# Two FFNs and linear attention on one core: expert coefficients moved by a unit, three chunks' queries taken from split z, state mask moved

## The chip, the cores and the metric

The kernel runs on one core of a Trainium2 chip. Its time is the device time of one execution in microseconds (us). Five engines work side by side and meet at semaphores: TensorE (PE, matmuls and, as PEld, weight loads), VectorE (DVE), ScalarE (ACT), GpSimd (POOL) and SyncE (SP), which issues DMAs.

## The reference, cut to what matters

Four blocks follow each other, each on a layer norm of the running sum `x` (4 x 1024 tokens of 256 numbers): a state space block, an FFN with product keys, a linear attention, and the same FFN again.

```
x = x + mamba(layernorm(x))
x = x + ffn(layernorm(x))
x = x + attn(layernorm(x))
x = x + ffn(layernorm(x))

ffn: queries = (z @ W_q).reshape(2, n, 64)           # n = 4096 tokens
     routing = einsum('tnd,tdk->tnk', queries, keys)   # top 8 of 64 keys, twice
     scores, indices = top 8 of the 64 sums
     ew  = silu(z . down_embed[indices]) * softmax(scores)
     out = (silu(z @ gate_w) * (z @ up_w)) @ down_w + ew @ up_embed[indices]

attn: q, k = relu(z @ Wq) / 4, relu(z @ Wk) / 4;  v = z @ Wv;  u = silu(z @ Wu)
      kv  = k^T v per head (16 heads of 16)
      out = (srms_norm(q kv) * u) @ Wo
```

The reshape to (2, n, 64) is what couples the chunks: the first half of all tokens gives the first key half's queries, the second half the others.

## The kernel before, in words

`res` holds `x` in SBUF throughout. An FFN works on eight chunks (`c`) of 512 tokens. `z` is the normalised and transposed chunk in two parts, a rounded high part and the rest, so that a product takes three fast matmuls (`split_mm`, format fp32r) for each block of 128 rows.

A chunk has twelve units (`i`, KM = 12). Units 0 to 7 (KH = 8) are hidden columns: PE makes the gate (psG) and the up projection (psU), ACT the silu, DVE the product (`product`, L1412), ACT rounds it (`high`, L1276), DVE makes the rest (`low`, L1417). Units 8 to 11 are the 512 experts: gate is the product with down_embed, and into psU PE transposes the expert coefficients C (L1197). The two buffers of psG, psU, sil and prod alternate. Then the down projection (L1234) runs in two halves, and DVE adds each to `res` (L1459). Behind the first half PE turns the next chunk's z (`turn`).

The coefficients come about beside units 0 to 7. Route scores are made from `qs` behind unit 0, DVE finds the highest (`highest`), ACT makes the exponentials at unit 3, DVE normalises them (`normalise_softmax`), POOL spreads them over 8 x 64 (W, L1108), and DVE masks W and corrects one entry (`coefficients`: four L1397, L1404, L1405), which raises C_ready. On DVE this stood behind `product(6)` and `low(5)`:

```
for i in range(KM):
    product(c, i)
    if i > 0: low(c, i - 1)
    ...
    if i == KH - 2: coefficients(c)
```

The queries of chunk pair s and s + 4 serve the routes of chunks 2s and 2s + 1. Chunks 0, 1, 4 and 5 of the first FFN and 0 and 4 of the second have theirs made by the block before. The others are asked inside earlier chunks (table ASKED): DVE normalises the chunk once more (`question`), PE turns it at unit 1 (L1167, eight transposes), ACT copies it (L1291), PE multiplies with W_q at unit 3 in full precision (`asked`, L1172, two matmuls of 512 columns), and ACT keeps the result in QT. The buffers lie in W's space, so that POOL's W waits for the question.

The chunks with a question were loops on PE, ACT and partly POOL, those without another loop, the last ones straight code.

In attention a looped sequence on DVE (`sequence`) gates and squares two halves, scales the first (`scale(b, 0)`, L1872), scales the second, which waits for POOL's inverse norms (L1601), and masks the next sequence's state to its heads (`keep_kv`, L1851). PE waits for that state ahead of output 0 (L1706), since output and state share the accumulator `acc`.

Of the kernel before, what the change touches and what calls it, by code (L numbers as in the profile page):

```python
# [14 lines left out]
P = 128  # L15
# [955 lines left out]
class Between:  # L971


    def __init__(self, nc, sb):
        at = nc.sbuf_base
        self.SW = sb("SW", [P, 2, TILES * TOP * KEYS])
        self.z = nc.alloc_sbuf_tensor_at("z_att", [P, 2, KD, SEQ], FP32R, offset=at)
        self.zn = sb("zns", [P, 2, TILES, D])


# [24 lines left out]
def ffn(nc, res, dram, name, shared, between, norms, first, out=None):  # L1005

    ASKED = {1: 2, 2: 6, 3: 3, 4: 7} if first else {0: 1, 1: 5, 2: 2, 3: 6, 4: 3, 5: 7}
    ctx = ExitStack()  # L1010
    with ctx:
# [18 lines left out]
        top1 = sb("top1", [P, TILES, 2, TOP])  # L1030
        sums = sb("sums", [P, TILES, TOP, TOP])
        top2 = sb("top2", [P, TILES, TOP])
# [57 lines left out]
        def _(pool):  # L1090
# [6 lines left out]

            def chunk(c, n=None):
# [6 lines left out]
                if n is not None:  # L1105
                    pool.wait_ge(q_full, n + 1)
# [14 lines left out]
            if first:  # L1121
                low(2)
                chunk(0)
                pool.wait_ge(C_ready, 1)
                low(3)
                inverse(2, 1)
                inverse(3, 2)
                chunk(1, 0)
                inverse(6, 3)
                chunk(2, 1)  # L1130
                inverse(7, 4)
                with pool.Fori(3, 5) as c:
                    chunk(c, c - 1)
                with pool.Fori(5, CHUNKS) as c:
                    chunk(c)
                pool.wait_ge(next_var, 1)
                at = slice(0, SEQ_TILES)
                pool.tensor_tensor(norms.inv[:, at, 0], norms.var[:, at], mhalf[:, 0:SEQ_TILES],
                                   ALU.pow).then_inc(next_inv, 1)
            else:  # L1140
                chunk(0, 0)
# [3 lines left out]
                with pool.Fori(1, 6) as c:  # L1145
                    chunk(c, c)
                with pool.Fori(6, CHUNKS) as c:
                    chunk(c)

        @block.tensor  # L1150
        def _(pe):
# [22 lines left out]

            def turn(c, n):

                pe.wait_ge(zn_ready, c)
                if n is not None:
                    pe.wait_ge(QT_ready, n + 1)
                turned(psX, zn).then_inc(turn_full, 1)  # L1180
# [19 lines left out]

            def chunk(c, more, n=None):
                pe.wait_ge(z_ready, c + 1)
                start = first and isinstance(c, int) and c == 0
                for i in range(KM):
# [3 lines left out]
                    if i == 0:  # L1208
# [7 lines left out]
                        last.then_inc(route_full, 1)  # L1216
                    if i == 1 and n is not None:
                        pe.wait_ge(zq_ready, n + 1)
                        pe.wait_ge(Rt_ready, c + 1)
                        turned(psX, zq).then_inc(turnq_full, 1)  # L1220
                    if i == 3 and n is not None:
                        pe.wait_ge(zT_ready, n + 1)
                        asked(psX[:, 0, :], zT).then_inc(q_full, 1)
                if start:
                    pe.wait_ge(w_low, 2)
                for i in range(2):
# [13 lines left out]
                    if i == 0 and more:  # L1240
                        turn(c + 1, n)

            if first:
                chunk(0, True)
                with pe.Fori(1, 5) as c:
                    chunk(c, True, c - 1)
                with pe.Fori(5, CHUNKS - 1) as c:
                    chunk(c, True)
            else:
                with pe.Fori(0, 6) as c:  # L1250
                    chunk(c, True, c)
                chunk(6, True)
            chunk(CHUNKS - 1, False)

        @block.scalar
        def _(act):
# [20 lines left out]

            def chunk(c, more, n=None, k=None):
                for i in range(KM):
# [9 lines left out]
                    if i == 2 and k is not None:  # L1289
                        act.wait_ge(turnq_full, n + 1)  # L1290
# [4 lines left out]
                    if i == 4 and k is not None:  # L1295
                        act.wait_ge(q_full, n + 1)
                        keep(k, psX[:, 0, :])
                    if i == 6 and first and not more:
# [9 lines left out]
                if more:  # L1308
                    prepare(c + 1, None if k is None else n + 1)
                    high_z(c + 1)  # L1310

            if first:
                prepare(0, None)
                chunk(0, True)
                with act.Fori(0, 2) as b:
                    chunk(2 * b + 1, True, 2 * b, b + 2)
                    chunk(2 * b + 2, True, 2 * b + 1, b + 6)
                with act.Fori(5, CHUNKS - 1) as c:
                    chunk(c, True)
            else:  # L1320
                prepare(0, None)
                with act.Fori(0, 3) as b:
                    chunk(2 * b, True, 2 * b, b + 1)
                    chunk(2 * b + 1, True, 2 * b + 1, b + 5)
                chunk(6, True)
            chunk(CHUNKS - 1, False)

        @block.vector
        def _(dve):
# [90 lines left out]
            def chunk(c, more, prepare=None, early=None):  # L1420
                for i in range(KM):
# [47 lines left out]
            if first:  # L1469
                def start_second():  # L1470
                    statistics(2)
                    statistics(3)
                    question(2, 0, 1)

                def start_third():
                    statistics(6)
                    question(6, 1, 3)

                def start_fourth():
                    statistics(7)  # L1480
                    question(3, 2, 2)

                chunk(0, True, start_second)
                chunk(1, True, start_third)
                chunk(2, True, start_fourth)
                chunk(3, True, lambda: question(7, 3, 4))
                chunk(4, True)
                with dve.Fori(5, CHUNKS - 1) as c:
                    own.enter(c - 5, 9)
                    chunk(c, True)  # L1490
                    own.leave(CHUNKS - 6)
            else:
                def late_statistics():
                    own.link(token_statistics(nc, own, norms, res, stats, mv4, pause, CHUNKS - 1))
                    nc.vector.tensor_scalar(norms.var[:, LATE_TILES], norms.mv[:, LATE_TILES, 1], EPS, None,
                                            ALU.add).then_inc(var_ready, 1)

                question(1, 0, None)
# [5 lines left out]
                chunk(5, True)  # L1504
                chunk(6, True)
            chunk(CHUNKS - 1, False)
# [7 lines left out]
def attention(nc, res, dram, norms, shared, between):  # L1514
# [5 lines left out]
    with ctx:  # L1520
# [303 lines left out]
        def _(dve):  # L1824
# [203 lines left out]
```

## Time and profile before

| | us |
|---|---|
| median of 3 runs | 1921.82 |
| lowest, highest | 1918.57, 1923.24 |
| the profiled execution, its own time | 1917.6 |
| its span in the profile | 1915.9 |
| mean granted clock of TensorE | 0.971 |

A timeline row gives start, duration, engine, line, operation and tiles (written <- read), how many instructions of one kind it merges, and in brackets the engine's idle time ahead of it and what ended that. Matmuls are pipelined: their durations overlap, and their pace is to be read from the starts. In a table by stretch the granted clock is a share of 2.4 GHz. The state space block ends some 912 us into the span, the first FFN at 1318, attention at 1508.

### The profile page before, as it was taken

To read this page: it belongs to the slowest core of one execution; us is meant where nothing else is said; L and a number is where in the kernel's file an instruction comes from. 1 tells how busy PE (TensorE), PEld (TensorE's weight loads), DVE (VectorE), ACT (ScalarE), POOL (GpSimd) and SP (SyncE) were. 2 spreads that over 40 slices of the span, in tenths; PEclk is the share of its full clock that TensorE was granted. 3 is DMA by queue.
4 is the path that set the end of the run, shared out by engine and by line. 5 is a ranking of instruction groups with operands and counts; after the bars stand their busy time and mean duration, and the time that the engine had idled before them with its cause. 6 is when DMAs were issued, how large, how long until landed. Compare 5 with 4: busy or idle time off the path is not lost. (4 is left out here: it accounts for less than half of the span.)

```text
span 1915.9 us, 26914 instructions
## 1 busy us (share of the span) xinstructions
PE 1756.1 (92%) x9643; PEld 1385.4 (72%) x9643; DVE 1435.7 (75%) x2217; ACT 1083.5 (57%) x1870; POOL 1061.3 (55%) x633
## 2 busy tenths in 40 slices
PE   6888989898998989767999999999999899999999
PEld 2556666665656666656788888888888688888888
DVE  4799999999999999999766656664444755555565
ACT  6777786878787876777344333342333443333433
POOL 3889999999999999999511111111445411111011
PEclk9898999999999999889999999999999999999999
DMA  6223332333333332261000000000000000000000
GB/s 195 85 80 106 100 100 94 95 105 92 105 92 102 104 101 92 79 208 50 1 1 1 0 0 1 1 22 6 1 0 1 1 11 11 11 11 11 11 12 12
DMA packets 59091, 101.11 MB, mean 53 GB/s; under 512 B 11120, under 2 KB 11248, under 8 KB 58864
## 3 DMA queue, kind: packets, MB, share of 16 engines
q1 hardware_dynamic: 58992, 99.88, 16.6%
q8 instruction: 51, 0.84, 0.2%
q14 instruction: 48, 0.39, 0.1%
HBM read 95.14 MB, written 4.72 MB: 52 GB/s over the span
## 5 line engine op out<-in xcount | busy, mean ns | idle before, releaser
L383 POOL TENSOR_TENSOR m_U<-m_U,m_C 128x1024 f32<-128x1024 f32 x255 | 600.8, 2369 | 25.7 <-DVE m_U L890 15.5
L525 PEld LDWEIGHTS m_y<-ident,m_U 128*128 128x128 f32 x2048 | 252.4, 148 | 118.1 <-issue 70.9
L890 DVE TENSOR_TENSOR_SCAN m_U<-m_dA,m_carry,m_U 128x512 f32<-128x512 f32 x256 | 311.4, 1272 | 5.2 <-ACT m_dA L758 4.8
L525 PE MATMUL m_y<-ident,m_U 128*128 128x128 f32 x2048 | 284.7, 285 | 30.4 <-POOL m_U L383 30.3
L890 DVE TENSOR_TENSOR_SCAN m_U<-m_dA,m_U 128x512 f32<-128x512 f32 x256 | 296.5, 1209 | 11.5 <-ACT m_dA L758 8.2
L758 ACT ACTIVATE m_dA<-high,m_negA 128x512 f32<-128x512 f32 x256 | 172.4, 685 | 71.5 <-DVE m_U L890 71.0
L758 ACT ACTIVATE m_dA<-even,m_negA 128x512 f32<-128x512 f32 x256 | 170.7, 684 | 54.1 <-DVE m_U L890 53.0
L1102 POOL TENSOR_TENSOR SW<-g_Rt 128x1024 f32<-128x1024 f32 x16 | 31.6, 1997 | 258.3 <-ACT g_Rt L1287 258.3
L1282 ACT ACTIVATE g_sil<-g_psG 128x512 f32<-128x512 f32 x96 | 57.6, 600 | 156.1 <-PE g_psG L1161 155.9
L1282 ACT ACTIVATE f_sil<-f_psG 128x512 f32<-128x512 f32 x96 | 57.5, 599 | 151.3 <-PE f_psG L1161 150.8
L1102 POOL TENSOR_TENSOR SW<-f_Rt 128x1024 f32<-128x1024 f32 x16 | 31.6, 1997 | 190.6 <-ACT f_Rt L1287 190.6
L506 PE MATMUL m_psB<-m_stack,m_pick 128*128 128x512 f32 x196 | 100.7, 514 | 35.0 <-DVE m_U L873 34.6
L873 DVE TENSOR_TENSOR m_U<-even,m_psB 128x1024 f32<-128x1024 f32 x100 | 120.3, 1203 | 11.2 <-PE m_psB L506 11.0
L1161 PE MATMUL f_psG<-zs,weights_hi 128*128 128x512 f32 x384 | 124.3, 405 | 2.5 <-DVE f_pause L1468 2.5
L1161 PE MATMUL g_psG<-zs,weights_hi 128*128 128x512 f32 x384 | 124.7, 406 | 1.4 <-DVE g_pause L1468 1.4
L873 DVE TENSOR_TENSOR m_U<-high,m_psB 128x1024 f32<-128x1024 f32 x96 | 115.6, 1204 | 4.2 <-PE m_psB L506 4.2
L415 PE MATMUL m_job<-turned 128*128 128x512 f32 x224 | 107.6, 603 | 3.8 <-issue 3.5
L1412 DVE TENSOR_TENSOR zns<-g_psU,g_sil 128x512 f32<-128x512 f32 x96 | 66.3, 690 | 59.6 <-PE g_psU L1161 50.8
L1234 PE MATMUL f_psO<-weights_hi,f_H_hi 128*128 128x256 f32 x384 | 109.2, 284 | 0.4 <-POOL weights_lo L1116 0.3
L1234 PE MATMUL g_psO<-weights_hi,g_H_hi 128*128 128x256 f32 x384 | 108.8, 283 | 0.0
L1234 PE MATMUL g_psO<-weights_lo,g_H_hi 128*128 128x256 f32 x384 | 107.3, 280 | 0.0
L1234 PE MATMUL f_psO<-weights_lo,f_H_hi 128*128 128x256 f32 x384 | 107.3, 280 | 0.0
(369 smaller groups left out, 4383.2 us busy)
## 6 DMA issues: line engine op xcount, KB each, us to landing
m_C<-bc_rows SPq DMA_DIRECT2D x256, 256.0 KB, 3.2
m_B<-bc_rows SPq DMA_DIRECT2D x60, 256.0 KB, 3.6
even<-in_ffn_w SPq DMA_DIRECT2D x16, 256.0 KB, 4.9
out<-res SPq DMA_DIRECT2D x8, 512.0 KB, 2.8
res<-in_x SPq DMA_DIRECT2D x1, 3072.0 KB, 13.4
res<-in_x SPq DMA_DIRECT2D x2, 512.0 KB, 4.3
turned<-in_Wkvqu SPq DMA_DIRECT2D x1, 1024.0 KB, 4.8
high<-in_in_w SPq DMA_DIRECT2D x1, 512.0 KB, 4.6
```

What stands on the lines that cost most here:

```text
L383: pool.tensor_tensor(u, u, C[:, M % C_RING, :].unsqueeze(1).to_broadcast([P, PE_E, CHUNK]), ALU.mult).then_inc(hc_ready, 1)
L415: ins = nc.tensor.matmul(out, w, x, start=first and k == 0, stop=last and k == len(pairs) - 1)
L506: nc.tensor.matmul(psB[:, :], pick[:, n:n + 1].to_broadcast([P, P]), stack[:, q, :], start=True, stop=True).then_inc(B_full, 1)
L525: last = nc.tensor.matmul(y[:, t, j * P:(j + 1) * P], U[:, M % U_RING, j, t * P:(t + 1) * P], ident[:, :], start=False, stop=n == N - 1, i ...
L758: nc.scalar.activation(dA[:, s % A_RING, :], delta[q][:, e, :], ACT.Exp, scale=negA[:, e, n:n + 1]).then_inc(dA_ready, 1)
L873: nc.vector.tensor_tensor(U[:, M % U_RING, :, :], dx[q][:, pair(p), :], psB[:, :].unsqueeze(1).to_broadcast([P, PE_E, CHUNK]), ALU.mult).t ...
L890: nc.vector.tensor_tensor_scan(u, dA[:, s % A_RING, :], u, carry[:, e, n:n + 1] if q else 0.0, ALU.mult, ALU.add).then_inc(scan_done, 1)
L1102: pool.tensor_tensor(S[:, 2 * b:2 * b + 2, :, :], Rt[:, b, 0, :, 0:TOP].unsqueeze(3).to_broadcast([P, 2, TOP, KEYS]), Rt[:, b, 1, :, :].un ...
L1161: last = nc.tensor.matmul(out, a, b, start=n == 0, stop=n == len(terms) - 1)
L1234: last = nc.tensor.matmul(psO[:, i, h * D:(h + 1) * D], H[a][:, k, j * P:(j + 1) * P], lower[b][:, k, :], start=m == 0, stop=m == len(term ...
L1282: nc.scalar.activation(sil[:, i % 2, :], psG[:, i % 2, :], ACT.Silu).then_inc(g_free, 1)
L1412: nc.vector.tensor_tensor(prod[:, i % 2, :], psU[:, i % 2, :], sil[:, i % 2, :], ALU.mult).then_inc(u_free, 1)
```

## The change

1. `coefficients(c)` on DVE stands behind `product(5)` and `low(4)`.
2. Questions: three chunks' queries in the second FFN (1, 2, 3) and two in the first (2, 3) are made while that chunk is worked on, from its own z parts: six split matmuls (`asked_own`) behind unit 5 into psX's second bank, copied by ACT at unit 6. W_q gets a high and a low part for it once (`wqs`). The others (6, 7 in the first FFN; 5, 6, 7 in the second) are still turned.
3. Chunks 0 to 4 are written out on PE, ACT and POOL; a loop runs over 5 and 6. `sums` uses the space of `qs`. Statistics and inverse roots of the first FFN's later chunks are made in another order.
4. In attention the mask of the state stands between the two scalings.

```diff
-    ASKED = {1: 2, 2: 6, 3: 3, 4: 7} if first else {0: 1, 1: 5, 2: 2, 3: 6, 4: 3, 5: 7}
+    TURNED = {1: 6, 3: 7} if first else {1: 5, 3: 6, 4: 7}
+    OWN = (2, 3) if first else (1, 2, 3)
+    BEHIND = 5
...
+            def asked_own(out):
+                terms = [(between.wqs[:, i, k, :], z[j][:, k, :]) for k in range(KD) for i, j in ((0, 0), (0, 1), (1, 0))]
+                for n, (a, b) in enumerate(terms):
+                    last = nc.tensor.matmul(out, a, b, start=n == 0, stop=n == len(terms) - 1)
+                return last
...
-                    if i == 3 and n is not None:
-                        pe.wait_ge(zT_ready, n + 1)
+                    if i == 3 and turns(c):
+                        pe.wait_ge(zT_ready, turned_in(c) + 1)
                         asked(psX[:, 0, :], zT).then_inc(q_full, 1)
+                    if i == 5 and own_asks(c):
+                        asked_own(psX[:, 1, :]).then_inc(q_full, 1)
...
+            for c in range(BEHIND):
+                chunk(c, True)
+            with pe.Fori(BEHIND, CHUNKS - 1) as c:
+                chunk(c, True)
             chunk(CHUNKS - 1, False)
...
+                    if i == 6 and own_asks(c):
+                        act.wait_ge(q_full, asked_in(c + 1))
+                        keep(c, psX[:, 1, :])
...
+                nc.scalar.activation(between.wqs[:, 0, :, :], wq, ACT.Copy)
...
-                    if i == KH - 2:
+                    if i == KH - 3:
                         coefficients(c)
...
+                def low_wq():
+                    dve.wait_ge(qs_ready, 1)
+                    nc.vector.tensor_tensor(between.wqs[:, 1, :, :], wq, between.wqs[:, 0, :, :].bitcast(FP32),
+                                            ALU.subtract)
...
+                def end_first():
+                    statistics_of(2, 6)
+                    question(6, 0, 2)
+
+                chunk(0, True, end_first, low_wq)
+                chunk(1, True, lambda: statistics_of(3, 7))
+                chunk(2, True, lambda: question(7, 1, 4), lambda: dve.wait_ge(inv_ready, 3))
...
-                question(1, 0, None)
-                chunk(0, True, lambda: question(5, 1, 1), late_statistics)
-                chunk(1, True, lambda: question(2, 2, None))
-                chunk(2, True, lambda: question(6, 3, None))
-                chunk(3, True, lambda: question(3, 4, None))
-                chunk(4, True, lambda: question(7, 5, None))
+                chunk(0, True, lambda: question(5, 0, 1), late_statistics)
+                chunk(1, True)
+                chunk(2, True, lambda: question(6, 1, None))
+                chunk(3, True, lambda: question(7, 2, None))
...
                 scale(b, 0)
+                keep_kv(b + 1)
                 scale(b, 1)
-                keep_kv(b + 1)
```

How it stands on the engines. DVE in a chunk of the second FFN, units 4 to 7, before (L1412 is `product`, L1417 `low`, L1397 to L1405 `coefficients`):

```order
L1412 TENSOR_TENSOR zns<-g_psU,g_sil 128x512
L1417 TENSOR_TENSOR g_H_lo<-zns,g_H_hi 128x512
L1412 TENSOR_TENSOR zns<-g_psU,g_sil 128x512
L1417 TENSOR_TENSOR g_H_lo<-zns,g_H_hi 128x512
L1412 TENSOR_TENSOR zns<-g_psU,g_sil 128x512
L1417 TENSOR_TENSOR g_H_lo<-zns,g_H_hi 128x512
L1397 SCALAR_TENSOR_TENSOR SW,g_csum<-SW,g_top 128x512 x4
L1404 TENSOR_TENSOR SW<-SW,g_csum 128x4
L1405 TENSOR_SCALAR SW<-SW 128x4
L1412 TENSOR_TENSOR zns<-g_psU,g_sil 128x512
```

The same stretch after (L1429 is now `product`, L1434 `low`, L1414 to L1422 `coefficients`):

```order
L1429 TENSOR_TENSOR zns<-g_psU,g_sil 128x512
L1434 TENSOR_TENSOR g_H_lo<-zns,g_H_hi 128x512
L1429 TENSOR_TENSOR zns<-g_psU,g_sil 128x512
L1434 TENSOR_TENSOR g_H_lo<-zns,g_H_hi 128x512
L1414 SCALAR_TENSOR_TENSOR SW,g_csum<-SW,g_top 128x512 x4
L1421 TENSOR_TENSOR SW<-SW,g_csum 128x4
L1422 TENSOR_SCALAR SW<-SW 128x4
L1429 TENSOR_TENSOR zns<-g_psU,g_sil 128x512
L1434 TENSOR_TENSOR g_H_lo<-zns,g_H_hi 128x512
```

One pair of product and low, that of units 6 and 5, has moved from ahead of the coefficients to behind them.

DVE in the looped attention sequence, before:

```order
L1844 TENSOR_TENSOR z_att<-a_acc,z_att 128x512
L1876 ISA
L1872 TENSOR_TENSOR a_og<-a_og,a_rinv 128x256 x4
L1876 REGISTER_ALU
L1877 REGISTER_ALU
L1872 TENSOR_TENSOR a_og<-a_og,a_rinv 128x256 x4
L1849 REGISTER_ALU
L1851 TENSOR_TENSOR a_kvh<-a_acc,a_same_head 128x128 x2
L1883 ISA
```

And after:

```order
L1891 ISA
L1887 TENSOR_TENSOR a_og<-a_og,a_rinv 128x256 x4
L1864 REGISTER_ALU
L1866 TENSOR_TENSOR a_kvh<-a_acc,a_same_head 128x128 x2
L1891 REGISTER_ALU
L1892 REGISTER_ALU
L1887 TENSOR_TENSOR a_og<-a_og,a_rinv 128x256 x4
L1898 ISA
```

The two masking instructions stand ahead of the second four scalings.

## Rows read from the trace of the kernel before

**Rows 1.** The page's first part: busy us (share), instructions; one line of it.

```profile
PE 1756.1 (92%) x9643; PEld 1385.4 (72%) x9643; DVE 1435.7 (75%) x2217; ACT 1083.5 (57%) x1870; POOL 1061.3 (55%) x633
```

**Rows 2.** Groups of instructions on PE: busy us, mean ns, idle before and releaser.

```profile
L1197 PE MATMUL g_psU<-ident,SW 128*128 128x128 f32 x128 | 19.4, 274 | 4.4 <-DVE SW L1405 4.4
```

**Rows 3.** Timeline of PE, second FFN, chunk 1: start us, duration us, instruction.

```profile
1585.13 0.62 PE L1161 MATMUL g_psG<-zs,weights_hi 128*128 128x512 f32 x2
...
1586.26 0.39 PE L1161 MATMUL g_psG<-zs,weights_lo 128*128 128x512 f32 x1
1587.20 0.63 PE L1197 MATMUL g_psU<-ident,SW 128*128 128x128 f32 x4 [0.55 <-DVE SW L1405]
...
1588.83 0.40 PE L1161 MATMUL g_psG<-zs,weights_lo 128*128 128x512 f32 x1
1589.06 0.60 PE L1197 MATMUL g_psU<-ident,SW 128*128 128x128 f32 x4
```

**Rows 4.** Timeline of DVE at the same place.

```profile
1580.91 0.68 DVE L1417 TENSOR_TENSOR g_H_lo<-zns,g_H_hi 128x512 fp32r<-128x512 f32 x1
1582.66 0.69 DVE L1412 TENSOR_TENSOR zns<-g_psU,g_sil 128x512 f32<-128x512 f32 x1 [1.07 <-PE g_psU L1161]
...
1583.87 0.74 DVE L1397 SCALAR_TENSOR_TENSOR SW<-SW,g_top 128x512 f32<-128x512 f32 x1
...
1586.88 0.17 DVE L1405 TENSOR_SCALAR SW<-SW 128x4 f32<-128x4 f32 x1
```

**Rows 5.** Timeline of POOL, then of DVE, first FFN, chunk 6.

```profile
1233.98 3.63 POOL L1108 TENSOR_TENSOR SW<-f_ex 128x2048 f32<-128x2048 f32 x1 [5.82 <-DVE f_ex L1390]
...
1235.79 2.36 DVE L1417 TENSOR_TENSOR f_H_lo<-zns,f_H_hi 128x512 fp32r<-128x512 f32 x1
...
1238.89 0.68 DVE L1417 TENSOR_TENSOR f_H_lo<-zns,f_H_hi 128x512 fp32r<-128x512 f32 x1
```

**Rows 6.** Timeline of PE: first coefficient transposes of five chunks.

```profile
1195.92 0.63 PE L1197 MATMUL f_psU<-ident,SW 128*128 128x128 f32 x4 [0.55 <-DVE SW L1405]
...
1244.45 0.63 PE L1197 MATMUL f_psU<-ident,SW 128*128 128x128 f32 x4 [0.55 <-DVE SW L1405]
...
1536.00 0.63 PE L1197 MATMUL g_psU<-ident,SW 128*128 128x128 f32 x4 [0.55 <-DVE SW L1405]
...
1840.51 0.63 PE L1197 MATMUL g_psU<-ident,SW 128*128 128x128 f32 x4 [0.55 <-DVE SW L1405]
...
1889.04 0.63 PE L1197 MATMUL g_psU<-ident,SW 128*128 128x128 f32 x4 [0.55 <-DVE SW L1405]
```

**Rows 7.** Timeline of PE, then of DVE, attention, around output 0.

```profile
1365.96 0.71 PE L1644 MATMUL a_acc<-a_kv 128*128 128x128 f32 x4
...
1370.04 6.68 PE L1706 MATMUL a_acc<-a_wo,a_ogT 128*128 128x256 f32 x16 [2.92 <-DVE a_kvh L1851]
...
1412.72 0.71 PE L1644 MATMUL a_acc<-a_kv 128*128 128x128 f32 x4
...
1417.09 5.36 PE L1706 MATMUL a_acc<-a_wo,a_ogT 128*128 128x256 f32 x16 [3.22 <-DVE a_kvh L1851]
...
1458.43 0.71 PE L1644 MATMUL a_acc<-a_kv 128*128 128x128 f32 x4
...
1462.41 3.72 PE L1706 MATMUL a_acc<-a_wo,a_ogT 128*128 128x256 f32 x16 [2.84 <-DVE a_kvh L1851]
...
1367.98 1.43 DVE L1872 TENSOR_TENSOR a_og<-a_og,a_rinv 128x256 f32<-128x256 f32 x4 [9.06 <-POOL a_rinv L1601]
1369.33 0.48 DVE L1851 TENSOR_TENSOR a_kvh<-a_acc,a_same_head 128x128 f32<-128x128 f32 x2
```

**Rows 8.** Busy time by stretch: us; PE, PEld, DVE, ACT, POOL; granted clock; DMA.

```profile
1370.00:1377.00 7.00, 6.96 (x18) 5.64 (x19) 0.81 (x2) 0.00 (x0) 0.00 (x0) 0.57 0.00 0
```

**Rows 9.** Timeline of POOL, first FFN, end of chunk 0.

```profile
956.72 1.25 POOL L1096 TENSOR_TENSOR inv<-var,f_mhalf 128x4 f32<-128x4 f32 x1 [1.09 <-DVE var L1347]
```

**Rows 10.** Who waited for whom: us in total, times, longest us.

```profile
DVE res L1459 <- PE f_psO L1234: 75.3, 14, 6.3
```

More of the change, by code:

```diff
@@ L978, in __init__ @@
         self.zn = sb("zns", [P, 2, TILES, D])
+        self.wqs = sb("wqs", [P, 2, KD, P], FP32R)
 class Norms:
@@ L1005, in ffn, with turned_in, asked_in, asks @@
 def ffn(nc, res, dram, name, shared, between, norms, first, out=None):
-    ASKED = {1: 2, 2: 6, 3: 3, 4: 7} if first else {0: 1, 1: 5, 2: 2, 3: 6, 4: 3, 5: 7}
+    TURNED = {1: 6, 3: 7} if first else {1: 5, 3: 6, 4: 7}
+    OWN = (2, 3) if first else (1, 2, 3)
+    BEHIND = 5
+    def turned_in(c):
+        return len([b for b in TURNED if b < c])
+    def asked_in(c):
+        return turned_in(c) + len([b for b in OWN if b < c])
+    def asks(c):
+        return isinstance(c, int) and (c in TURNED or c in OWN)
+    def turns(c):
+        return isinstance(c, int) and c in TURNED
+    def own_asks(c):
+        return isinstance(c, int) and c in OWN
     ctx = ExitStack()
@@ L1096, in inverse, with chunk @@
                 pool.tensor_tensor(norms.inv[:, at, 0], norms.var[:, at], mhalf[:, 0:TILES], ALU.pow).then_inc(inv_ready, 1)
-            def chunk(c, n=None):
+            def chunk(c):
                 pool.wait_ge(Rt_ready, c + 1)
@@ L1126, in _ @@
                 inverse(2, 1)
[L1127 to L1130, printed above, removed]
+                inverse(6, 2)
+                chunk(1)
+                inverse(3, 3)
                 inverse(7, 4)
-                with pool.Fori(3, 5) as c:
-                    chunk(c, c - 1)
-                with pool.Fori(5, CHUNKS) as c:
+                for c in range(2, BEHIND):
+                    chunk(c)
+                with pool.Fori(BEHIND, CHUNKS) as c:
                     chunk(c)
@@ L1140, in _ @@
             else:
-                chunk(0, 0)
+                chunk(0)
                 pool.wait_ge(var_ready, 1)
@@ L1144, in _ @@
                                    ALU.pow).then_inc(inv_ready, 1)
-                with pool.Fori(1, 6) as c:
-                    chunk(c, c)
-                with pool.Fori(6, CHUNKS) as c:
+                for c in range(1, BEHIND):
+                    chunk(c)
+                with pool.Fori(BEHIND, CHUNKS) as c:
                     chunk(c)
@@ L1173, in asked, with turn @@
                 return last
-            def turn(c, n):
+            def asked_own(out):
[3 more added lines that the diff above has]
+                return last
+            def turn(c):
                 pe.wait_ge(zn_ready, c)
-                if n is not None:
-                    pe.wait_ge(QT_ready, n + 1)
+                if isinstance(c, int) and asks(c - 1):
+                    pe.wait_ge(QT_ready, asked_in(c))
                 turned(psX, zn).then_inc(turn_full, 1)
@@ L1199, in hidden, with chunk @@
                 last.then_inc(u_full, 1)
-            def chunk(c, more, n=None):
+            def chunk(c, more):
                 pe.wait_ge(z_ready, c + 1)
@@ L1240, in chunk @@
                     if i == 0 and more:
[L1241 to L1252, printed above, removed]
+                        turn(c + 1)
+            for c in range(BEHIND):
+                chunk(c, True)
+            with pe.Fori(BEHIND, CHUNKS - 1) as c:
+                chunk(c, True)
             chunk(CHUNKS - 1, False)
@@ L1276, in high, with chunk @@
                 nc.scalar.activation(H[0][:, i, :], prod[:, i % 2, :], ACT.Copy).then_inc(hi_ready, 1)
-            def chunk(c, more, n=None, k=None):
+            def chunk(c, more):
                 for i in range(KM):
@@ L1288, in chunk @@
                                              ACT.Copy).then_inc(Rt_ready, 1)
-                    if i == 2 and k is not None:
-                        act.wait_ge(turnq_full, n + 1)
+                    if i == 2 and turns(c):
+                        act.wait_ge(turnq_full, turned_in(c) + 1)
                         nc.scalar.activation(zT, psX[:, :, :], ACT.Copy).then_inc(zT_ready, 1)
@@ L1294, in chunk @@
                         nc.scalar.activation(ex[:, :, :], ex[:, :, :], ACT.Exp).then_inc(exp_ready, 1)
-                    if i == 4 and k is not None:
-                        act.wait_ge(q_full, n + 1)
-                        keep(k, psX[:, 0, :])
+                    if i == 4 and turns(c):
+                        act.wait_ge(q_full, asked_in(c) + 1)
+                        keep(TURNED[c], psX[:, 0, :])
+                    if i == 6 and own_asks(c):
+                        act.wait_ge(q_full, asked_in(c + 1))
+                        keep(c, psX[:, 1, :])
                     if i == 6 and first and not more:
@@ L1308, in chunk @@
                 if more:
-                    prepare(c + 1, None if k is None else n + 1)
+                    prepare(c + 1, asked_in(c + 1) if asks(c) else None)
                     high_z(c + 1)
             if first:
[L1313 to L1325, printed above, removed]
+                nc.scalar.activation(between.wqs[:, 0, :, :], wq, ACT.Copy)
+            prepare(0, None)
+            for c in range(BEHIND):
+                chunk(c, True)
+            with act.Fori(BEHIND, CHUNKS - 1) as c:
+                chunk(c, True)
             chunk(CHUNKS - 1, False)
@@ L1469, in _, with statistics_of @@
             if first:
[L1470 to L1486, printed above, removed]
+                def low_wq():
+                    dve.wait_ge(qs_ready, 1)
+                    nc.vector.tensor_tensor(between.wqs[:, 1, :, :], wq, between.wqs[:, 0, :, :].bitcast(FP32),
+                                            ALU.subtract)
+                def statistics_of(k, n):
+                    statistics(k)
+                    statistics(n)
+                def end_first():
[4 more added lines that the diff above has]
+                chunk(2, True, lambda: question(7, 1, 4), lambda: dve.wait_ge(inv_ready, 3))
+                chunk(3, True)
                 chunk(4, True)
@@ L1496, in late_statistics @@
                                             ALU.add).then_inc(var_ready, 1)
-                question(1, 0, None)
-                chunk(0, True, lambda: question(5, 1, 1), late_statistics)
-                chunk(1, True, lambda: question(2, 2, None))
-                chunk(2, True, lambda: question(6, 3, None))
-                chunk(3, True, lambda: question(3, 4, None))
-                chunk(4, True, lambda: question(7, 5, None))
-                chunk(5, True)
-                chunk(6, True)
+                chunk(0, True, lambda: question(5, 0, 1), late_statistics)
+                chunk(1, True)
+                chunk(2, True, lambda: question(6, 1, None))
+                chunk(3, True, lambda: question(7, 2, None))
+                for c in range(4, CHUNKS - 1):
+                    chunk(c, True)
             chunk(CHUNKS - 1, False)
```

10 lines of the change are left out of this document (5 added, 5 removed).

## The prediction

> **What bounds the kernel now.** I read the share of busy time first [rows 1]: TensorE (PE) is busy 92% of the span, so a change pays only where it gives PE less to do or takes away a wait of PE's. Next come PE's groups of instructions, to see which of them stand behind idle time, and then the timeline of PE and its partner at those places. In both FFNs PE runs without a gap except once per chunk, ahead of the coefficient transposes L1197: 4.4 us over eight chunks of the second FFN, released by VectorE (DVE) [rows 2]. The reader should see in [rows 3] how large that stall is. The last gate matmul of unit 8 starts at 1586.26 and the transposes at 1587.20, 0.94 us later; one unit on, where nothing waits, the same step takes 1589.06 - 1588.83 = 0.23 us. So 0.71 us are lost, in each of the 16 chunks alike (every first transpose row names the same 0.55 us of idle time, five of them in [rows 6]). In attention PE stands still ahead of output 0 (L1706) in each of the three looped sequences: 2.92, 3.22 and 2.84 us, all released by the masked state kvh (L1851) [rows 7].
>
> **Part 1, coefficients one unit sooner.** On DVE the block of four L1397, L1404 and L1405 moves ahead of product(6) and low(5). In chunk 1 of the second FFN low(5) and the block follow product(6), which starts at 1582.66; the block runs from 1583.87 to 1586.88 + 0.17 = 1587.05, 3.18 us, and PE starts 0.15 us after that [rows 4]. Placed behind low(4), it starts at 1580.91 + 0.68 = 1581.59 and ends at 1584.77; product(6) ends 0.69 us later, at 1585.46. PE now wants both at 1587.20 - 0.71 = 1586.49, so 1.0 us is spare. The tighter case is a chunk without a question. In chunk 6 of the first FFN low(4) starts at 1238.89 [rows 5]; the block ends at 1238.89 + 0.68 + 3.18 = 1242.75, product(6) at 1243.44, and PE wants them at 1244.45 - 0.71 = 1243.74 [rows 5, 6]. 0.3 us is spare. GpSimd's (POOL's) multiplication, on which the block waits, ends at 1233.98 + 3.63 = 1237.61 against a wish at 1239.57. What queues behind the block on DVE is product(6), and behind product(6) on ScalarE (ACT) the copy high(6) and then silu(8); PE asks for silu(8) only at unit 10, two units (about 1.8 us each there, [rows 3]) later. I take the full 16 x 0.71 = **11.4 us**; the lower bound is 0 if the stall only changes its name.
>
> The row at 1235.79 shows why DVE is late there: a subtraction with two operands in SBUF takes 2.36 us beside POOL's multiplication, against 0.68 us elsewhere [rows 5]. The Trainium skill, SBUF - State Buffer, section "SBUF: two separate sides", calls the port pair of VectorE and GpSimd an exclusive lock for such operations; the trace agrees. By that rule the weights' low parts, which POOL makes in chunk 0 of the first FFN as soon as the coefficients are there, now meet other DVE instructions; it stays a matter of that one chunk.
>
> **Part 2, queries from the own z parts.** Before, ten chunks (four and six) turn and ask one question each: eight transposes L1167 and two full-precision matmuls L1172. The price stands in the distance of neighbouring chunks [rows 3, 6]: with a question 1587.20 - 1536.00 = 51.20 us, without one 1889.04 - 1840.51 = 48.53 us, so 2.67 us of PE per question. After, five are left, and five are asked by six split matmuls of 512 columns. Such matmuls start every (1586.26 - 1585.13) / 5 = 0.226 us [rows 3], so six cost 1.36 us. The sum is 5 x (2.67 - 1.36) = **6.6 us**. As the chunks are PE-bound outside the one stall, all of it is on the path. DVE loses five times four normalisations and ACT five copies, which is off the path and gives nothing. Into the chunks with an own question 1.36 us come between units 5 and 6, where they give DVE more time for the coefficients. New at the start are one ACT copy and one small DVE subtraction of wq; both lie beside PE work, price 0.
>
> At the end of chunk 0 of the first FFN DVE now waits for two inverse roots instead of one before it normalises question 6. The second runs for 1.25 us from 956.72 [rows 9], so DVE waits some 1.5 us, and behind it stand the first addition to res and z's low part. In such places DVE waits up to 6.3 us for PE's down projection anyway [rows 10], and z is wanted a whole half projection later. Price 0, upper bound 1.5 us.
>
> **Part 3, state masked between the two scalings.** PE's last accumulation of the state ends at 1365.96 + 0.71 = 1366.67; DVE is idle then, but the mask stands behind the second scaling, which waits for POOL until 1367.98 [rows 7]. With the mask ahead: PE to DVE I set like DVE to PE, 1370.04 - (1369.33 + 0.48) = 0.23 us, so the state is there for PE at 1366.67 + 0.23 + 0.48 + 0.23 = 1367.61. The first half of the output wants nothing else but the ogT copy that the first transposed half left behind before the last accumulation. Gain 1370.04 - 1367.61 = 2.43 us, and in the same way 1417.09 - 1414.37 = 2.72 and 1462.41 - 1460.08 = 2.33: **7.5 us**. The second scaling still waits for POOL, not for the mask, so it isn't later; who reads it is PE behind four query groups.
>
> Behind two of the three gaps the same 16 matmuls take 6.68 and 5.36 us instead of 3.72 [rows 7], and the granted clock from 1370 to 1377 is 0.57 [rows 8]: PE ran at the lower level, 1.2 GHz, after it had idled. With some 0.5 us of idle left I expect no fall there; that gives back 2.96 + 1.64 = **4.6 us**. Other executions may have lost less or more; bounds 0 and 3 x 2.96 = 8.9.
>
> **Code written out.** The chunks 0 to 4 lose their loops on PE, ACT and POOL. In the trace a chunk reached by a jump back (1195.92 to 1244.45, 48.53 us) and one in straight code (1840.51 to 1889.04, 48.53 us) are equally long [rows 6], so I price this at 0. The Trainium skill, Runtime: NRT & Kernel Launch, section "Instruction fetch mechanics", says that a taken branch out of the fetched pages stalls the engine while sequential fetch is hidden. By that rule the seven jumps back that PE no longer takes would be a further gain; the trace shows none.
>
> **Sum.** 11.4 + 6.6 + 7.5 + 4.6 = 30.1 us. Against the profiled execution, 1917.6 us, that gives 1887.5. The median shown is 4.2 us longer, 1921.8, and that is what will be compared: 1921.8 - 30.1 = **1891.7 us**, 1.6% faster.
>
> **Rivals.**
> A. The stall changes its name: PE waits for product(6) or silu behind it. For it: only 0.3 us spare in nine chunks without any question. Against it: 1.0 us and more in the others. 9 x 0.71 = 6.4 us come back, 1898.1; all sixteen, 1903.1. Chance 0.12.
> B. Attention gives nothing or little: PE waits for the ogT copy or for POOL, and the clock falls all the same. Up to 12.1 us come back, 1903.8; the clock alone, 4.6, gives 1896.3. Against it: the mask is the only releaser named. Chance 0.12.
> C. The straight code costs: PE, with five chunks written out per FFN, runs out of fetched instructions. Nine chunk bodies that stood in loops are now straight code; from 30.1 / 9 = 3.3 us per body the kernel is slower than before. With 4 us per body, 36 us, it takes 1927.6. Against it: the equal 48.53 us. Chance 0.03.
> D. The jumps did cost something that I can't see between equal chunks. With as much as one coefficient stall, 0.71 us, for each of seven, 5.0 us more are gained: 1886.7. The page on the runtime named above would lead one there. Chance 0.05.
> E. DVE's new order is late for the down projection as well, and A and B come together: 1905 to 1915. Chance 0.04.
>
> **How the numbers follow.** The forecast, 0.64, covers 1887 to 1897 (clock part between 0 and its upper bound). The range goes from 1886 (D) to 1904 (A and B whole), and leaves out C, E and some executions' scatter. A measurement tells 0.3%, 5.8 us, from no change; all but C, and a trace of E, are faster by more. Faster 0.95, same 0.02, slower 0.03.
>
> **What would show it.** In the changed trace: first coefficient transposes 47.8 us apart in chunks without a question, 49.2 with an own one, and no idle time named in front of them; L1706's line with under 0.7 us of idle time and 16 matmuls in 3.7 us, three times; on DVE the mask right behind the first scaling. Wrong would be: idle time ahead of the transposes with ACT or DVE product as releaser (A), a granted clock under 1.00 behind output 0 (B), PE idle by "issue" inside chunks 1 to 4 (C).

## The result and the profile after

| | before | after |
|---|---|---|
| median, us | 1921.49 (4 executions, 1918.57 to 1923.24) | 1887.35 (4 executions, 1886.89 to 1888.0) |
| ratio | | 0.983, 95% interval 0.9817 to 0.9843 |
| profiled execution / its span | 1917.6 / 1915.9 | 1887.3 / 1885.6 |
| mean granted clock | 0.971 | 0.974 |

The kernel is 34.1 us faster by the medians, and the two profiled executions differ by 30.3 us. Forecast were 1891.7 us and 30.1 us less; 1887.35 lies in the range of 1886 to 1904.

The first five lines of who waited for whom on PE, changed kernel, from the first FFN on (total us, times, longest us). No line for the coefficient transposes is among them; before, PE was idle for 4.4 us ahead of them in the second FFN alone [rows 2]:

```profile
PE a_ring L1711 <- DVE a_og L1887: 4.2, 2, 2.4
PE f_psG L1181 <- DVE f_pause L1485: 2.5, 1, 2.5
PE g_psG L1181 <- DVE g_pause L1485: 1.3, 1, 1.3
PE a_ring L1638 <- DVE a_pause L1954: 1.3, 1, 1.3
PE a_acc L1721 <- DVE a_kvh L1866: 0.9, 3, 0.3
```

PE's timeline: the first coefficient transposes of chunks 5, 6 and 7 of the second FFN, with the matmul ahead of one of them (start us, duration us). To be read beside [rows 3, 6]:

```profile
1763.22 0.60 PE L1222 MATMUL g_psU<-ident,SW 128*128 128x128 f32 x4
...
1810.78 0.40 PE L1181 MATMUL g_psG<-zs,weights_lo 128*128 128x512 f32 x1
1811.01 0.60 PE L1222 MATMUL g_psU<-ident,SW 128*128 128x128 f32 x4
...
1858.80 0.60 PE L1222 MATMUL g_psU<-ident,SW 128*128 128x128 f32 x4
```

The step from the matmul to the transposes is 0.23 us where it was 0.94, and chunks without a question follow at 47.79 us where it was 48.53. On DVE the same place of chunk 6, with POOL's multiplication ahead of it, beside [rows 4, 5]:

```profile
1801.24 3.63 POOL L1129 TENSOR_TENSOR SW<-g_ex 128x2048 f32<-128x2048 f32 x1 [5.82 <-DVE g_ex L1407]
...
1806.15 0.68 DVE L1434 TENSOR_TENSOR g_H_lo<-zns,g_H_hi 128x512 fp32r<-128x512 f32 x1
...
1806.75 0.75 DVE L1414 SCALAR_TENSOR_TENSOR SW<-SW,g_top 128x512 f32<-128x512 f32 x1
...
1809.76 0.17 DVE L1422 TENSOR_SCALAR SW<-SW 128x4 f32<-128x4 f32 x1
1809.87 0.69 DVE L1429 TENSOR_TENSOR zns<-g_psU,g_sil 128x512 f32<-128x512 f32 x1
```

Product(6) ends at 1810.56 and PE takes the transposes at 1811.01: 0.45 us from end to start. The step from DVE's last instruction to PE took 0.15 us where PE waited for it [rows 4], so about the 0.3 us of room that the prediction counted is there. The place is narrow, but it holds. Attention, timeline of DVE and PE around output 0, beside [rows 7]:

```profile
1358.20 0.49 DVE L1866 TENSOR_TENSOR a_kvh<-a_acc,a_same_head 128x128 f32<-128x128 f32 x2 [7.80 <-PE a_acc L1659]
...
1400.84 1.43 DVE L1887 TENSOR_TENSOR a_og<-a_og,a_rinv 128x256 f32<-128x256 f32 x4 [0.98 <-POOL a_rinv L1616]
...
1357.45 0.71 PE L1659 MATMUL a_acc<-a_kv 128*128 128x128 f32 x4
...
1358.91 3.71 PE L1721 MATMUL a_acc<-a_wo,a_ogT 128*128 128x256 f32 x16 [0.31 <-DVE a_kvh L1866]
...
1400.09 3.72 PE L1721 MATMUL a_acc<-a_wo,a_ogT 128*128 128x256 f32 x16 [0.32 <-DVE a_kvh L1866]
...
1441.26 3.72 PE L1721 MATMUL a_acc<-a_wo,a_ogT 128*128 128x256 f32 x16 [0.32 <-DVE a_kvh L1866]
```

The gaps of 2.92, 3.22 and 2.84 us are 0.31 to 0.32 us, and the 16 matmuls take 3.71 to 3.72 us each time. The granted clock there, by stretch, is the number 1.00 behind the engines' busy times, beside [rows 8], where it was 0.57:

```profile
1357.00:1363.00 6.00, 5.69 (x33) 4.85 (x32) 2.83 (x8) 1.59 (x4) 2.33 (x1) 1.00 0.00 0
...
1440.00:1446.00 6.00, 5.68 (x30) 4.82 (x30) 3.55 (x10) 1.15 (x2) 1.68 (x1) 1.00 0.00 0
```

Cut into stages at PE's first matmul of each stage, the traces of all runs give this table (us; the last stage ends with the span). It carries most of what follows:

| kernel | first FFN starts at | first FFN | attention | second FFN |
|---|---|---|---|---|
| before | 915.01 | 403.95 | 189.51 | 407.43 |
| after | 914.97 | 395.49 | 176.76 | 398.38 |
| mask alone (e1) | 915.36 | 404.04 | 175.17 | 407.43 |
| coefficients alone (e2) | 916.83 | 397.86 | 189.37 | 401.54 |
| after, mask back (e3) | 914.80 | 395.62 | 187.84 | 398.34 |
| straight code alone (e4) | 915.41 | 403.93 | 192.39 | 407.47 |
| after again (e5) | 915.63 | 395.60 | 176.77 | 398.30 |
| after, coefficients back (e6) | 915.06 | 401.50 | 175.07 | 404.37 |
| after, coefficients two units sooner (e7) | 915.28 | 399.89 | 176.81 | 402.92 |
| e8, tail and statistics behind unit 7 | 916.13 | 395.47 | 172.99 | 399.11 |
| e9, tail alone | 916.66 | 395.48 | 173.00 | 398.36 |
| e10, tail and statistics at the end | 916.51 | 395.45 | 172.97 | 397.77 |
| before again (e11) | 915.11 | 403.89 | 192.49 | 407.41 |

### The profile page after: what moved, and what is told of

Read it like the earlier page. It is cut to its first block and busy times, and to the rows that moved or that the text cites. A ratio compares the mean times of both kernels' runs of the same rounds, so it can differ in the third digit from the quotient of the medians.

```text
span 1885.6 us, 26501 instructions
## 1 busy us (share of the span) xinstructions
PE 1742.8 (92%) x9613; PEld 1381.1 (73%) x9613; DVE 1432.4 (76%) x2198; ACT 1079.3 (57%) x1866; POOL 1060.5 (56%) x633
## 5 line engine op out<-in xcount | busy, mean ns | idle before, releaser
L525 PE MATMUL m_y<-ident,m_U 128*128 128x128 f32 x2048 | 284.8, 285 | 30.3 <-POOL m_U L383 30.2
L873 DVE TENSOR_TENSOR m_U<-even,m_psB 128x1024 f32<-128x1024 f32 x100 | 119.7, 1197 | 11.2 <-PE m_psB L506 11.0
L1261 PE MATMUL f_psO<-weights_hi,f_H_lo 128*128 128x256 f32 x384 | 107.1, 279 | 0.0
```

The lines of the kernel that those rows point to most:

```text
L525: last = nc.tensor.matmul(y[:, t, j * P:(j + 1) * P], U[:, M % U_RING, j, t * P:(t + 1) * P], ident[:, :], start=False, stop=n == N - 1, i ...
L873: nc.vector.tensor_tensor(U[:, M % U_RING, :, :], dx[q][:, pair(p), :], psB[:, :].unsqueeze(1).to_broadcast([P, PE_E, CHUNK]), ALU.mult).t ...
L1261: last = nc.tensor.matmul(psO[:, i, h * D:(h + 1) * D], H[a][:, k, j * P:(j + 1) * P], lower[b][:, k, :], start=m == 0, stop=m == len(term ...
```

## The experiments

### Each part by itself

The theory after the result: the three parts add up on PE, and the 3.8 us by which the medians fell further than the profiled executions belong to attention, where the clock falls differently from execution to execution. The rival gives them to the FFNs.

**e1, the mask alone.**

```diff
                 scale(b, 0)
-                scale(b, 1)
                 keep_kv(b + 1)
+                scale(b, 1)
```

> The kernel before with part 3 alone: the state mask between the two scalings. Theory: the 3.8 us by which the median fell further than the profiled executions (34.1 against 30.3) belong to this part, since executions of the kernel before lose TensorE's clock behind one, two or three of the three long gaps. Then the median comes to 1921.5 - 12.1 - 3.8, about 1905.6, and the executions lie within some 1.5 us of each other instead of 4.7. Rival: the part is worth only what the two profiled executions showed, 12.1 us: 1909.4, with the scatter of before; the other 3.8 us then belong to the FFNs.

Measured: 1905.82 us (five executions, 1902.77 to 1906.7) against 1920.53 us of before on that chip (15 executions), ratio 0.9921, interval 0.9907 to 0.9934. That is 14.7 us less than before on its own chip, between the rival's 12.1 and the theory's 15.9 and nearer the theory. The other half of the theory fell: the executions still lie 3.9 us apart. So the long gaps aren't the only thing that makes executions differ.

**e2, the coefficients alone.**

```diff
-                    if i == KH - 2:
+                    if i == KH - 3:
                         coefficients(c)
```

> The kernel before with part 1 alone: coefficients one unit sooner. Theory: 16 x 0.71 = 11.4 us less than before, 1910.1, with the scatter of before kept (the gaps in attention are still there), and no idle time named ahead of the transposes. Rival: part of the stall comes back in chunks without a question, where only 0.3 us was spare: up to 6.4 us less gain, 1916.5.

Measured: 1907.36 us (five executions), ratio 0.9927, interval 0.9914 to 0.9941, 13.2 us less. By the stages, the first FFN is 6.09 us shorter and the second 5.89, 12.0 us in all. No idle time is left ahead of the transposes; the rival of the chunks with little to spare is out.

**e3, the changed kernel with the mask put back** (the edit of e1 undone).

> The changed kernel with the mask put back behind the second scaling. Theory: everything of part 3 comes back, gaps of 2.9 us three times and the clock falls behind some of them: 1887.4 + 15.9 = 1903.3 in the median, with executions up to 5 us apart again. Rival: 1899.5 (12.1 us), scatter as in the changed kernel, about 1 us.

Measured: 1899.09 us (four executions, 1897.99 to 1901.02), ratio 0.989, interval 0.9875 to 0.9905. That is 11.7 us above the changed kernel's first median (11.0 above its second, e5, below), so here the rival's number is met and the theory's is missed by 4 us, while e1 came nearer the theory's. The scatter of 3.0 us fits neither. In the traces attention is 11.1 us longer. PE's timeline of e3, output 0 three times, with the gap ahead of it in brackets:

```profile
1361.48 5.40 PE L1721 MATMUL a_acc<-a_wo,a_ogT 128*128 128x256 f32 x16 [2.91 <-DVE a_kvh L1866]
...
1407.12 5.16 PE L1721 MATMUL a_acc<-a_wo,a_ogT 128*128 128x256 f32 x16 [3.12 <-DVE a_kvh L1866]
...
1452.27 3.72 PE L1721 MATMUL a_acc<-a_wo,a_ogT 128*128 128x256 f32 x16 [2.82 <-DVE a_kvh L1866]
```

The gaps are back in full; the clock took 1.7, 1.4 and 0 us this time.

**e4, the loops written out, nothing else.** `with pe.Fori(1, 5) as c:` becomes `for c in range(1, 5):`, and likewise the other loops over chunks with a question on PE, ACT and POOL.

```diff
-                with pe.Fori(0, 6) as c:
+                for c in range(0, 6):
                     chunk(c, True, c)
```

> The kernel before with only its loops over chunks with a question written out on TensorE, ScalarE and GpSimd; nothing else is changed. Theory: no difference, 1921.5 within 1.5 us, and first coefficient transposes 51.2 us apart as before. Rival 1 (the jumps back cost something): shorter, up to 5 us. Rival 2 (straight code runs out of fetched instructions): longer, by 3 us or more, with idle time named issue inside the chunks.

Measured: 1919.35 us (eleven executions) against 1920.53, ratio 0.9989, interval 0.998 to 0.9998. By the interval alone that is 0.4 to 3.8 us faster. But the FFNs, which are all that the edit touches, take 403.93 and 407.47 us against 403.95 and 407.43 in the traces, so they give it to nothing that was edited, and the small difference of the medians stays unexplained; the first transposes are 51.2 us apart as before, for instance chunks 1 and 2 of the second FFN:

```profile
1590.53 0.63 PE L1197 MATMUL g_psU<-ident,SW 128*128 128x128 f32 x4 [0.55 <-DVE SW L1405]
...
1641.71 0.63 PE L1197 MATMUL g_psU<-ident,SW 128*128 128x128 f32 x4 [0.55 <-DVE SW L1405]
```

By these stages both rivals of straight code (C and D) are out.

### Where the executions differ

**e5, the changed kernel again.**

> The changed kernel once more, unchanged. The medians fell by 34.1 us, the two profiled executions by 30.3. Theory: the executions of either kernel differ by some us in stages that the change doesn't touch (the state space block began the first FFN between 914.8 and 916.8 us in six traces) and behind the gaps left in attention, and the four executions of the changed kernel happened to be alike. Then this run scatters over 2 us or more and its median lies at 1887.5 to 1890. Rival: the changed kernel is steady, since its clock falls are gone: 1887.4, all executions within 1.2 us.

Measured: 1888.06 us (five executions, 1887.25 to 1889.06), before 1922.49 on that chip. On that chip the difference is 34.4 us, beside 34.1 in the result. Over all nine executions the changed kernel's median is 1887.65, within 2.2 us; over 37 executions on several chips the median of before is 1920.5, from 1917.23 to 1923.42. Pooled like that the difference is 32.9 us. The median is the first theory's; the scatter of 1.8 us lies between its 2 us and the rival's 1.2.

**e11, the kernel before, traced again** (no edit).

> The kernel before, unchanged, for a second trace of it. Theory: the state space block and attention differ from the first trace, the FFNs do not (403.95 and 407.43 us). With the clock fallen behind one, two or three gaps, attention takes 187 to 193 us, and the first FFN starts between 914.8 and 917 us; mean of attention in traces with the long gaps 189.8 us, so here most likely 190 to 191. Rival: attention is 189.5 us again and the execution, if longer than 1917.6 us, is so for another reason.

Measured: 1920.66 us, 3.1 us more than the first traced execution. The FFNs are equal to 0.06 us, attention is 192.49 instead of 189.51: inside the 187 to 193 us expected, above the 190 to 191 thought most likely. PE's timeline, the three outputs behind their gaps:

```profile
1370.06 6.76 PE L1706 MATMUL a_acc<-a_wo,a_ogT 128*128 128x256 f32 x16 [2.92 <-DVE a_kvh L1851]
...
1417.19 5.40 PE L1706 MATMUL a_acc<-a_wo,a_ogT 128*128 128x256 f32 x16 [3.23 <-DVE a_kvh L1851]
...
1462.56 6.59 PE L1706 MATMUL a_acc<-a_wo,a_ogT 128*128 128x256 f32 x16 [2.83 <-DVE a_kvh L1851]
```

The third output takes 6.59 us, where the first trace had 3.72 behind the same gap of 2.8 us. Against 3.72 us each, the slower clock cost the three outputs 7.6 us here and 4.6 us in the first trace; in e3, e2 and e4 it was 3.1, 4.5 and 7.6 us. So the first trace lies in the middle of five, and their mean is 5.5 us. In the five traces that have the long gaps attention takes 190.3 us in the mean (187.84 to 192.49), in the five without them and with the old tail 176.1 us (175.07 to 176.81). The difference is 14.2 us: 8.0 of gaps, 5.5 of clock behind them, and 0.7 because the clock also fell in attention's tail in all of the first five and in three of the other five (the last section shows it). That the mask's place has a part in this last 0.7 isn't shown.

### How much room the coefficients have

**e6, the changed kernel with the coefficients back** (the edit of e2 undone).

> The changed kernel with the coefficients put back behind unit 6. Theory: the one stall per chunk returns, 16 x 0.71 us and the share that hid in chunk 0 of either FFN: 11.4 to 12.0 us more than the changed kernel, 1899.4, each first transpose 0.94 us behind the matmul ahead of it. Rival: in the chunks with an own question the 1.36 us between units 5 and 6 hide part of it, so that only 11 chunks stall and 7.8 us return: 1895.2.

Measured: 1899.24 us (four executions), 11.2 us above e5. The stages lose 5.9 and 6.1 us. All sixteen chunks stall again, those with an own question too: those 1.36 us hide nothing, because DVE's order behind unit 6 is started later by just as much.

**e7, one more unit sooner.**

```diff
-                    if i == KH - 3:
+                    if i == KH - 4:
                         coefficients(c)
```

> The changed kernel with the coefficients behind unit 4, one more unit sooner. Theory (how narrow the place is): in the nine chunks without a question DVE reaches the block when GpSimd has just ended its multiplication, and product(5), now behind the block, is late for TensorE's up projection of unit 7 by about 1.2 us; chunks with a question have room. 9 x 1.2, about 11 us more: 1898. Rival: one unit more changes nothing, 1887.4, if the buffers give more room than I count.

Measured: 1897.28 us (four executions), 9.2 us above e5, near the theory's 11. Who waited for whom in it, on PE:

```profile
PE f_psU L1181 <- DVE zns L1429: 4.1, 5, 0.9
PE g_psU L1181 <- DVE zns L1429: 3.5, 4, 1.3
```

Nine waits, five and four, in exactly the chunks without a question, on product(5) that now stands behind the block. The distance of such chunks is 48.87 us against 47.78. Of the three places tried, behind units 4, 5 and 6, the one that the change picked is the only one without a stall.

### What the trace still shows

The changed kernel's second FFN gained less from part 2 than forecast. POOL, DVE and PE in its chunk 0 (start us, duration us):

```profile
1501.62 3.63 POOL L1129 TENSOR_TENSOR SW<-g_ex 128x2048 f32<-128x2048 f32 x1 [5.75 <-DVE g_ex L1407]
...
1503.31 1.97 DVE L1000 COPY mv<-g_mv 128x8 f32<-128x8 f32 x1
...
1505.42 0.69 DVE L1429 TENSOR_TENSOR zns<-g_psU,g_sil 128x512 f32<-128x512 f32 x1
...
1511.16 0.69 DVE L1429 TENSOR_TENSOR zns<-g_psU,g_sil 128x512 f32<-128x512 f32 x1
...
1506.16 0.73 PE L1181 MATMUL g_psU<-zs,weights_hi 128*128 128x512 f32 x2
...
1511.52 0.39 PE L1181 MATMUL g_psG<-zs,weights_lo 128*128 128x512 f32 x1
1511.91 0.66 PE L1222 MATMUL g_psU<-ident,SW 128*128 128x128 f32 x4
```

The late statistics stand behind unit 3, and a copy of eight numbers per partition takes 1.97 us beside POOL's multiplication, which ends at 1501.62 + 3.63 = 1505.25 (in e8 and e10, where nothing of POOL's runs beside it, the same copy takes 0.17 us); the first product behind it ends at 1506.11 and PE begins unit 6's up projection only then, and the transposes come 0.39 us behind the matmul ahead of them, not 0.23. Before, the 2.67 us of a question in this chunk covered that.

**e8, both leftovers.** The statistics move behind unit 7, and attention's last sequence gets another split of its inverse norms; DVE's order there changes with it, so that a copy and the Newton step stand ahead of the third and fourth scaling.

```diff
-            for t in range(TILES):
+            for t in range(2):
                 pool.wait_ge(ssq_ready, HALVES * (BATCH - 1) + t + 1)
...
-            late = slice(TILES, SEQ_TILES)
+            late = slice(2, SEQ_TILES)
...
-                        if early is not None:
+                        if early is not None and first:
                             early()
...
+                    if i == KH - 1 and early is not None and not first:
+                        early()
```

> The changed kernel with two stalls tackled that its trace still shows. The late statistics of the second FFN's chunk 0 move from behind unit 3 to behind unit 7 on VectorE (0.36 us of stall in that chunk), and in the last attention sequence GpSimd makes two inverse norms instead of four, the others go with the second half through ScalarE's logarithm and exponential and one Newton step (gaps of 1.8 and 2.4 us there, the second caused by GpSimd's 2.9 us each). Theory: 0.4 + 1.5 to 2 us, 1885.2. Rival: the first output half waits for something else at once (the zT copy on VectorE), no difference.

Measured: 1885.54 us (five executions, 1885.02 to 1886.59), ratio to before 0.9815, interval 0.9801 to 0.9829. Attention gains, the second FFN loses 0.7 us: behind unit 7 the statistics delay the product that the next transposes want, and PE waits 0.6 us for it.

**e9, the tail alone** (the last two edits of e8 undone).

> The changed kernel with only the tail of attention changed: two inverse norms on GpSimd instead of four, the rest on ScalarE's path; the late statistics stand behind unit 3 again. Theory: behind unit 7 the statistics cost the second FFN 0.7 us (399.11 against 398.4 us in the traces), and the tail alone gains 2.1 to 3.8 us: 1885.54 - 0.7 = 1884.8. Rival: the difference between the FFN times is of another kind, 1885.5.

Measured: 1883.89 us (five executions, 1883.3 to 1885.64). Attention takes 173.00 us. The second transposing of the tail, in the changed kernel and then in e9:

```profile
1473.76 0.44 PE L1711 MATMUL a_ring<-ident,a_og 128*128 128x128 f32 x2 [2.36 <-DVE a_og L1887]
```

```profile
1473.13 0.68 PE L1711 MATMUL a_ring<-ident,a_og 128*128 128x128 f32 x4 [0.28 <-DVE a_og L1887]
```

The gap of 2.36 us is 0.28 us, and the clock no longer falls behind it in any of the three traces with the new tail.

**e10, the statistics at the end of chunk 0.**

```diff
-                chunk(0, True, lambda: question(5, 0, 1), late_statistics)
+                def end_of_first():
+                    late_statistics()
+                    question(5, 0, 1)
+
+                chunk(0, True, end_of_first)
```

> As the kernel with the tail alone, with the late statistics at the end of the second FFN's chunk 0, ahead of question 5. Theory: the stall of 0.54 us in chunk 0 goes (first transposes 24.15 us after the stage's start instead of 24.69), and the wait for GpSimd's inverse roots lies beside the down projection: 1884.3. Rival: VectorE comes late to chunk 1's z low part, 0.5 us or more back.

Measured: 1884.41 us (five executions, 1882.68 to 1885.11). The second FFN's stage is 0.6 us shorter, 397.77 against 398.36, and its first transposes come 24.17 us after its start instead of 24.69, as expected; in the medians 0.5 us of the wrong sign is lost in the scatter. Both e9 and e10 lie below every execution of the changed kernel (1886.89 at the least), but on another chip, whose before was at 1919.18. Against the before measured with them they are 35.3 and 34.8 us faster, the changed kernel was 34.1 and 34.4 us, so the medians leave open how much of the 3 to 4 us is the chip. In the traces attention is 3.8 us shorter than in the changed kernel. DVE's new order in the tail and the new split were not tried one without the other. Which of e9 and e10 is faster stays open in the medians, and the trace says e10.

## Why the prediction was right, point by point

**Part 1, 11.4 us forecast, 12.0 measured** (e2, by stages; e6 undone gives 12.0 again). The stall per chunk was sized right: 48.53 - 47.79 = 0.74 us per chunk against 0.71. The 0.3 us of room in chunks without a question were enough, and e7 shows how little more there was. The exclusive lock on the shared ports (the Trainium skill, SBUF - State Buffer, section "SBUF: two separate sides") was named for the first FFN's chunk 0 and left at price 0, rightly: e2's first FFN gained no less than its second. What did cost time is the copy in the second FFN's chunk 0, 1.97 us beside POOL's multiplication instead of 0.17, which agrees with the rule and which the prediction did not look at.

**Part 2, 6.6 us forecast, 5.5 measured** (changed kernel less e2: 2.37 and 3.16 us). This is the term that was mis-sized. An own question costs 49.21 - 47.79 = 1.42 us, not 1.36, 0.3 us over five; and the step "As the chunks are PE-bound outside the one stall, all of it is on the path" failed in the second FFN's chunk 0, where taking the question away uncovered DVE's late statistics: 0.5 us, which e10 gave back. The other 0.2 us are not traced. They may lie in the first FFN, where the first transposes of chunks 0 and 1 are 51.50 us apart and in e2 51.40; the prediction had priced a wait for a second inverse root there at 0, with 1.5 us as its bound.

**Part 3, 7.5 + 4.6 us forecast.** The gaps gave 8.0 us, since the way from PE to DVE is shorter than the 0.23 us assumed for it: PE's last accumulation ends at 1357.45 + 0.71 = 1358.16 and the mask starts at 1358.20. In the first pair of traces the other 4.7 us are clock, so 12.75 us in all. Over ten traces it is 14.2 us: the clock's share was taken from one execution, 4.6 us, and is 5.5 us in the mean of five, from 3.1 to 7.6. The prediction's bounds of 0 and 8.9 us held it.

**Written out code, 0 us forecast**: e4's FFN stages agree with the kernel before to 0.04 us. The rule of the Trainium skill, Runtime: NRT & Kernel Launch, section "Instruction fetch mechanics", by which a taken branch can stall the engine, doesn't show with these loop bodies.

**The base.** The forecast of the gain, 30.1 us, matched the traced pair, 30.3, to 0.2 us. That is partly luck: part 1 and the gaps gave 1.1 us more than forecast and part 2 gave 1.1 us less, and the clock's 4.6 us had been read from one of the two traces compared. For the median that gain was taken from 1921.8, and the measured median lies 4.3 us under the forecast. Part 3 explains 1.5 to 2 us of that. By the stages the sum is 12.0 + 5.5 + 14.2 = 31.7 us; the medians differ by 32.9 us pooled and by 34.1 and 34.4 us in the two direct comparisons, so 1.2 to 2.7 us aren't explained. The state space block, which no edit touches, began the first FFN between 914.80 and 916.83 us in the thirteen traces, so stages outside the change move by as much.

## What to carry to other kernels

On an engine that is busy 92% of the time, look for the few places where it waits and move only the work behind which it waits; then check with one unit more whether the new place is an edge, as it was here. When work is taken off the bound engine, look at what that work had covered on the others. And before a clock effect is put into a sum, trace the unchanged kernel more than once: one trace gave 4.6 us for an effect that was 3.1 to 7.6 us in others.

## What the runs showed of the hardware

The same idle gap of 2.8 us ahead of the same 16 matmuls cost 0 us in one execution (3.72 us for them) and 2.9 us in another (6.59 us); gaps of 0.3 us, and one of 1.25 us at the start of attention, left the granted clock at 1.00 in every trace. The tail of attention with gaps of 1.8 and 2.4 us ran at either level: with the mask moved, attention took 175.1 us in two traces where the clock stayed up (e1, e6), and 176.8 us in three where it fell, one of them here, a stretch of the changed kernel with a granted clock of 0.76. In the five traces with the long gaps it fell there every time; with the new tail, where the gap of 1.8 us stands alone, it stayed up in all three:

```profile
1475.00:1482.00 7.00, 6.94 (x27) 4.95 (x25) 2.37 (x7) 2.72 (x4) 0.00 (x0) 0.76 0.01 2
```

The Trainium skill, TensorE: Matmul & The Clock Gate, section "What's actually happening", says that the throttled level is the default and activity releases it; the traces agree in that every fall between the first FFN's start and PE's last matmul stands at an idle gap of 1.8 us or more, and show besides that the same gap of 2.8 us brings it in one execution and not in the next. The gap's length alone doesn't decide: one of 2.5 us ahead of the first FFN, outside the change, was followed by the lower level in all thirteen traces (granted clock 0.57 from 915 to 919 us in the kernel before). Why, no run here tells.
